# Two layers on one core: second- and third-pass tasks interleaved, the MLP's second product one step later

## What is computed

```python
# layer 0
tgt1 = _layer_norm(tgt, g1, be1)
tgt = tgt + _self_attn(tgt1, mask, Wq, bq, Wk, bk, Wv, bv, Wo, bo)
tgt = tgt + (memory @ Wg.T + bg)
tgt1 = _layer_norm(tgt, g2, be2)
x = tgt + jax.nn.relu(tgt1 @ W1.T + b1) @ W2.T + b2
# layer 1
x = mha(layer_norm(x, ln1_s, ln1_b), ..., causal=True) + x
y = mha(layer_norm(x, ln2_s, ln2_b), encoded, ..., causal=False) + x
z = layer_norm(y, ln3_s, ln3_b)
out = y + jax.nn.relu(z @ mlp_w1 + mlp_b1) @ mlp_w2 + mlp_b2
```

## Time and profile before

| | us |
|---|---|
| median of 3 runs | 1721.41 |
| lowest and highest | 1719.3, 1725.6 |
| the profiled execution | 1704.09 |
| its span, first to last instruction | 1702.3 |
| mean granted TensorE clock, share of full | 0.956 |

### The profile page before, as it was taken

How to read it: one execution, slowest core, us unless ns; L and a number is a source line. 1 busy time by engine, 2 the same in 40 slices (tenths; PEclk the granted TensorE clock), 3 DMA queues, 4 the chain that set the end, 5 groups by cost and what they waited for, 6 DMA issues and landing times.

```text
span 1702.3 us, 42833 instructions
## 1 busy us (share of the span) xinstructions
PE 1459.5 (86%) x13376; PEld 1175.9 (69%) x13376; DVE 1212.1 (71%) x3855; ACT 1061.9 (62%) x2153; POOL 834.7 (49%) x1125
## 2 busy tenths in 40 slices
PE   2789999999998998878787777778999999999986
PEld 1567788877777887765566555555777777777756
DVE  2688887888878887656666766666776777677742
ACT  3677676777777775445565555556656665666552
POOL 3345454444444566544344443444555655565533
PEclk8799999999999999989899999998999999999989
DMA  5645555444544455444655646574644364546300
GB/s 145 139 113 119 108 109 118 99 99 105 117 100 99 105 125 130 119 107 107 124 121 111 129 101 140 115 153 93 119 112 105 99 128 99 105 101 129 79 26 13
DMA packets 163511, 185.75 MB, mean 109 GB/s; under 512 B 15952, under 2 KB 140240, under 8 KB 163408
## 3 DMA queue, kind: packets, MB, share of 16 engines
q1 hardware_dynamic: 163408, 184.57, 49.8%
HBM read 125.78 MB, written 58.72 MB: 108 GB/s over the span
## 4 chain that ended last, share of the span: by engine, by line
PE 42%; issue 13%; ACT 12%; DVE 12%; DMA 9%; POOL 6%; SPq 5%; ACTq 1%; DVEq 0%; POOLq 0%
PE d_ps L437 16%; PE d_ps L673 8%; DMA k_stack<-parts 7%; PE o_ps L572 5%; PE s_ps L494 5%; PE t_ps L542 3%; DVE prob L858 3%; PE t_ps L508 3%; SPq L399 2%; DMA parts<-q_part 2%; ACT prob_t L721 2%; SPq L404 2%; DVE o_n L890 2%; POOL h_lo L1031 2%; PE m_ps L444 1%
## 5 line engine op out<-in xcount | busy, mean ns | idle before, releaser
L721 ACT ACTIVATE prob_t<-t_ps 128x384 f32<-128x384 f32 (+1 forms) x512 | 275.4, 551 | 393.0 <-PE t_ps L542 197.7
L494 PE MATMUL s_ps<-k_stack,q_stack 96*128 96x256 bf16 (+1 forms) x1536 | 294.6, 275 | 124.5 <-DMA k_stack<-parts 47.5
L712 ACT ACTIVATE prob<-prob,neg_max 128x256 f32<-128x256 f32 x512 | 233.8, 514 | 121.0 <-DVE neg_max L858 118.8
L494 PEld LDWEIGHTS s_ps<-k_stack,q_stack 96*128 96x128 bf16 x1536 | 115.1, 100 | 227.8 <-issue 65.7
L542 PE MATMUL t_ps<-q_stack,k_stack 108*128 108x256 bf16 (+1 forms) x1024 | 207.3, 269 | 23.0 <-ACT prob_t L721 14.3
L858 DVE CUSTOM_DVE_ANT_0 prob<-s_ps,bias_sb 128x256 f32<-128x256 f32 x512 | 192.4, 416 | 48.5 <-PE s_ps L494 36.7
L858 DVE CUSTOM_DVE_ANT_0 prob<-s_ps,causal 128x128 f32<-128x128 f32 (+1 forms) x512 | 158.5, 352 | 90.2 <-PE s_ps L494 88.0
L843 DVE TENSOR_REDUCE top<-s_ps 128x2 f32<-128x512 f32 x256 | 172.9, 682 | 54.8 <-PE s_ps L494 51.3
L1031 POOL TENSOR_TENSOR h_lo<-h_f,h_hi 128x512 fp32r<-128x512 f32 x128 | 165.9, 1296 | 86.6 <-DVE h_hi L921 86.6
L572 PE MATMUL o_ps<-prob_t,v_sb 128*17 128x256 f32 (+1 forms) x3072 | 200.7, 381 | 0.0
L437 PE MATMUL d_ps<-x2t_hi,w_hi 128*128 128x256 f32 x512 | 157.0, 307 | 38.2 <-ACT k_f L780 21.8
(11 more groups left out here) (115 smaller groups left out, 4063.5 us busy)
## 6 DMA issues: line engine op xcount, KB each, us to landing
q_stack<-parts SPq DMA_DIRECT2D x288, 128.0 KB, 4.0
k_stack<-parts SPq DMA_DIRECT2D x288, 128.0 KB, 6.4
parts<-q_part SPq DMA_DIRECT2D x96, 192.0 KB, 2.3
parts<-k_part SPq DMA_DIRECT2D x96, 192.0 KB, 2.3
ct_kept<-ct_hl SPq DMA_DIRECT2D x16, 512.0 KB, 8.0
x_in<-x_mid SPq DMA_DIRECT2D x32, 256.0 KB, 2.9
x_res<-x_mid SPq DMA_DIRECT2D x32, 256.0 KB, 3.0
ct_hl<-ct_kept SPq DMA_DIRECT2D x16, 512.0 KB, 8.2
```

Source lines behind the costliest of these rows:

```text
L494: last = mm(s_ps[:, h % 2, q * S:q * S + n], q_stack[0:ROWS, t.par, HEAD[h], q * P:(q + 1) * P], k_stack[0:ROWS, t.par, HEAD[h], 0:n], sta ...
L712: last = nc.scalar.activation(prob[:, h % 4, q, :], prob[:, h % 4, q, :], ACT.Exp, bias=neg_max[:, h % 4, q:q + 1], scale=-1.0)
L721: nc.scalar.activation(prob_t[:, h % 8, 0:n], t_ps[:, h % 2, 0:n], ACT.Exp, scale=-1.0)\
```

## The change

**Order.** Tasks 0 to 15 are the first pass as before, 16 to 19 are the first four of the second pass. From task 20 on a second-pass task (sequence 4 + b) and a third-pass task (sequence b) take turns, to task 43; the last four are third-pass tasks. `Task` and `Step` are rewritten for a list of the order, `steps` has two loops in place of three, and the counts that each semaphore wait is for are worked out from the list.

**Weights.** Second-pass q/k/v weights get tiles of their own (`wx_hi`, `wx_lo`), and its output weights lie where the gate weights were. So both passes' weights are on chip at once. The stage tile is gone: early units are staged where the MLP's and the output's tiles lie later (`late`), the others in the first pass's probability tile. Units are loaded and split at other steps: unit 4 at step 1 in place of 14, units 8 and 9 at steps 18 and 19 in place of 30 and 32.

**The second MLP product.** For a third-pass task that is followed by a second-pass one (`late()`) W2 runs one step later than before, in slots 5, 6 and 8, its sum in slot 9, and its store in slot 9.

**Masks.** The causal mask and its bf16 twin are made at step 15 in the tile of the first pass's mask. The guard of the second pass writes its shifted scores, which nobody reads, into one shared tile, and waits for the guard before it.

The diff, cut:

```diff
-           (14, 12): (4,), (16, 13): (5,), (17, 9): (6,), (17, 14): (7,), (30, 12): (8,), (32, 13): (9,)}
+           (1, 5): (4,), (17, 2): (5,), (17, 10): (6,), (17, 15): (7,), (18, 9): (8,), (19, 3): (9,)}
-UNIT_LOAD_AT = {(-2, 2): 0, (-1, 0): 1, (-1, 14): 2, (0, 5): 3, (1, 0): 4, (15, 0): 5, (17, 1): 6, (17, 11): 7,
-                (18 - 1, 15): 8, (31, 0): 9}
+UNIT_LOAD_AT = {(-2, 2): 0, (-1, 0): 1, (-1, 14): 2, (0, 5): 3, (0, 14): 4, (16, 6): 5, (17, 4): 6, (17, 12): 7,
+                (18, 1): 8, (18, 12): 9}
-GATE_AT, W2_AT = 12, (11, 12, 14)
+GATE_AT, W2_AT, W2_LATE = 12, (11, 12, 14), (5, 6, 8)
+LEAD = 4
+ORDER = ([(0, b) for b in range(B)] + [(1, b) for b in range(LEAD)]
+         + [t for b in range(B - LEAD) for t in ((1, LEAD + b), (2, b))] + [(2, b) for b in range(B - LEAD, B)])
...
+    def late(self):
+        return self.p == 2 and self.pos + 1 < NTASK and ORDER[self.pos + 1][0] == 1
...
+        self.w2 = None
+        if self.old and self.old.p in MLP and not self.old.late():
+            self.w2 = self.old
+        elif self.older and self.older.late():
+            self.w2 = self.older
...
+        wx_hi, wx_lo = sb("wx_hi", [P, 3, KC, D], F32R), sb("wx_lo", [P, 3, KC, D], F32R)
...
-                if h in W2_AT and has(st.old, MLP):
-                    part = W2_AT.index(h)
+                at = (W2_LATE if st.w2.late() else W2_AT) if st.w2 else ()
+                if h in at:
+                    part = at.index(h)
                     if part == 0:
-                        weights(st.old, UNIT_W2)
-                        pe.wait_ge(h_done.sem, h_done.after(st.old, 3))
+                        weights(st.w2, UNIT_W2)
+                        if st.w2.late():
+                            pe.wait_ge(k_done.sem, k_done.after(st.nxt))
+                        pe.wait_ge(h_done.sem, h_done.after(st.w2, 3))
...
+                if t.p == 1:
+                    dve.sem_inc(passed, 1)
+                    last, hb = earlier_head(st, h, 1)
+                    dve.wait_ge(u_done.sem, u_done.after(last, hb + 1))
...
+                    shifted = spill[:, q, 0:n] if t.p == 1 else prob[:, h % 4, q, 0:n]
+                    last = v.tensor_tensor_reduce(shifted, s_ps[:, h % 2, q * S:q * S + n], bias,
...
-                if h == 15 and has(st.old, MLP):
-                    dve.wait_ge(w2_mm.sem, w2_mm.after(st.old))
+                if st.w2 and h == y_at(st.w2):
+                    t, before = st.w2, st.mlp_before(st.w2)
+                    dve.wait_ge(w2_mm.sem, w2_mm.after(t))
```

More of the change, by code:

```diff
@@ L104, in __init__, with mlp_before @@
         self.prev, self.old, self.older = at(-1), at(-2), at(-3)
+        self.w2 = None
[3 more added lines that the diff above has]
+            self.w2 = self.older
+    def mlp_before(self, task):
+        pos = task.pos - 1
+        while pos >= 0 and ORDER[pos][0] not in MLP:
+            pos -= 1
+        return Task(pos, task.i) if pos >= 0 or task.i is not None else None
 def steps(eng, body):
-    for s in range(-2, 2):
+    for s in range(-2, PAIRS_0):
@@ L119 @@
+    for s in range(NTASK - LEAD - 3, NTASK + 2):
+        body(Step(s))
 class Event:
@@ L144, in after @@
     def after(self, task):
[L146 to L148 removed]
+        n = sum(p in self.passes for p, _ in ORDER[task.par:task.pos + 1:2]) if task.pos >= 0 else 0
+        const = 16 * (self.dmas * n + self.credit)
+        return task.i * (16 * self.dmas) + const if task.i is not None and task.p in self.passes else const
 def two_layers(nc, x, ctx, mask, wa, wm1, wm2, cols, rows, ident, out):
@@ L193, in two_layers @@
         ident_bf = sb("ident_bf", [P, P], BF16)
-        later = sb("later", [P, P], BF16)
         one_hot = sb("one_hot", [P, CH])
@@ L545, in keyed_scores @@
                     if t.p == 1:
-                        last = mm(t_ps[:, h % 2, k * S:k * S + P], ident_bf[:, :], later[:, :], start=False, stop=True)
+                        last = mm(t_ps[:, h % 2, k * S:k * S + P], ident_bf[:, :], later, start=False, stop=True)
                 last.then_inc(st_mm.sem, 1)
@@ L799, in slot @@
                     act.wait_ge(w1_mm.sem, w1_mm.after(st.old, n + 1))
+                    if st.old.first and n == 0:
+                        act.wait_ge(unit_lo, 5)
                     if n >= 2:
```

236 lines of the change are left out of this document (134 added, 102 removed).

## The result

The changed kernel is slower: a median of 1739.1 us against 1717.0 us of the kernel before on the same chips, a ratio of 1.0118 with a 95% interval of 1.009 to 1.0145. The prediction, 1700 us, was wrong in its direction. Four of the changed kernel's 17 runs were over 1.5% above its fastest; they are in its median and not in the ratio.

A forecast was written before the change was run, and what follows sets the result against it. Second-pass steps were taken as ended by the k_stack transfer, third-pass steps as bound by TensorE. Terms of 800.4, 79.9, 618.0 and 182.9 us made a span of 1681.2, 21 less, hence a median of 1700 us; range 1664 to 1727.

The forecast's parts named there:

- What bounds the kernel before: Second-pass steps (27.0 us) end in a wait for the k_stack transfer; third-pass steps (34.0 us) are bound by TensorE.
- TensorE work: TensorE's busy time at full clock in the alternating steps: 25.3 us in A, 26.3 us in B.
- Idle time that B keeps: TensorE's idle time in B, built from the MLP-free step 1118.8 to 1144.7: 5.8 - 2.5 - 1.7 + 0.8 us.
- B: Alternating step whose current task is a third-pass one; forecast 28.7 us, 29.0 with the transfer's 0.3.
- Idle time that A keeps: TensorE's idle time in A: 2.1 + 0.8 + 0.7 us of waits and 0.7 for the layer norm.
- A: Alternating step whose current task is a second-pass one; forecast 29.6 us, 29.9 with the transfer's 0.3.
- The sum: Whole span: 800.4 us, steps 20 to 22 79.9, steps 23 to 43 618.0, the end 182.9; total 1681.2 us.
- the rival on the transfer: Transfer ends both kinds of alternating step and TensorE's clock falls: x = 31.2 us, total 1738 us; chance 0.14.
- x: Mean length of the 21 alternating steps, 23 to 43; the forecast's own range was 28.7 to 30.0 us.
- The transfer in B and A: Loads land 24.6 to 30.2 us into a step; late ones poke out by up to 1.4; 0.3 us a step added.
- The guard's added wait: Second-pass score guards, each waiting for the guard before: 0.1 us a step, bounds 0 and 54 us in all.
- Weights: Weight splits moved to steps 1, 18 and 19 hold GpSimd: 5 us taken, bounds 0 and 7.9 us.

The follow-up runs named there:

- b2: Kernel before with 44 of the 48 products of the third pass's second MLP product left out (output not the reference's); 1722.4 us, ratio 1.0014.
- d1: b2 with 16 products whose result nobody reads in slot 11 of third-pass steps; 1709.1 us, ratio 0.9961 to the kernel before.
- e3: Changed kernel with products nobody reads in slot 11 of steps 23 to 44, 10 in A and 16 in B; 1729.8 us, ratio 1.0074.
- e2: Changed kernel with one layer-norm normalisation on VectorE moved from slot 10 to slot 11; 1746.8 us, ratio 1.0189 to the kernel before.
- e4: Changed kernel with the late second MLP product in slots 9, 11 and 12 of A in place of 5, 6 and 8; 1744.5 us, ratio 1.0174.
- c1: Changed kernel with the first layer norm's statistics and variance moved from slots 9 and 10 to 4 and 5, steps 23 to 44; 1701.6 us, ratio 0.9918.
- f1: c1 with input normalisation in slot 9 (was 12), transposes in 11 (13), ScalarE's copies in 12 (14), steps 23 to 44; 1692.7 us, ratio 0.9866.
- b1: Kernel before with each second-pass score guard waiting for the guard before it, and nothing else; 1722.2 us, ratio 1.0029.
- b3: Kernel before with the first layer norm's statistics and variance moved from slots 9 and 10 to 4 and 5 in all steps; 1731.8 us, ratio 1.0071.
- d2: Kernel before with 16 products whose result nobody reads at the end of slot 15 in the second pass; 1709.0 us, ratio 0.9974.
- e1: Changed kernel with the second MLP product back in its old slots 11, 12 and 14, tasks still alternating; 1722.3 us, ratio 1.0041.
- c2: c1 with products nobody reads in slot 11 of steps 23 to 44, 6 in A and 5 in B; 1702.6 us, ratio 0.9933.
- f4: Changed kernel with ScalarE's four affine copies of the input in slot 13 in place of 14, steps 23 to 44; 1758.2 us, ratio 1.0235.
- f3: c1 with f1's edits and with weight splits moved to later slots; 1689.5 us, ratio 0.9838 to the kernel before.

## Why the prediction was wrong, by its steps

**What bounds the kernel before: right.** Second-pass steps ended in the transfer, and the change removed that: 25.8 us became 1.9.

**TensorE work: right.** 25.3 and 26.3 us forecast, 25.4 and 26.2 measured.

**Idle time that B keeps: the step that failed.** 2.4 us forecast, 5.0 measured. After the K copy (0.8 taken, 0.60 measured) 1.6 us were left for all the rest, read off the step at 1118.8:

```profile
1134.77 0.17 DVE L874 TENSOR_SCALAR ve<-mv 128x2 f32<-128x2 f32 x1
```

```profile
1135.59 0.39 PE L494 MATMUL s_ps<-k_stack,q_stack 96*128 96x256 bf16 x2 [0.54 <-DVE top L843]
1137.93 0.39 PE L494 MATMUL s_ps<-k_stack,q_stack 96*128 96x256 bf16 x2 [0.74 <-DVE top L843]
```

That step has no MLP at all: no activation to split, so no GpSimd instruction beside the variance add, which took 0.17 us, and no casts between the maxima. It also began behind a wait for the transfer, so that the one for the exponentials in slot 0 didn't show. B has them, and 3.3 us of waits in slots 12 and 13 (2.32, 0.74 and a last 0.25), besides 1.10 us in slot 0. The text said that W2 "covered VectorE's work there" and gave no price to it. The price is in b2 and d1: of 5.2 us of W2 1.1 come back at full clock, and none where the clock falls. In B itself TensorE has 5.8 us less to do than in the third-pass step (26.2 against 32.0), and at full clock B is 2.8 us shorter. The step to start from was the third-pass step of 34.0 us with all of VectorE's work of slots 9 to 13 laid end to end, and not one that lacks part of that work.

**Idle time that A keeps: about right, in other places.** 4.3 us (and 0.3 for the DMA) forecast, 4.9 measured. Slots 11 to 13 have 2.26 where 2.1 was taken; slot 0 has 1.29 for 0.74; the layer norm's 0.7 didn't come, and a wait of 0.77 for a `q_stack` copy in slot 15 did. The K copy cost 0.28 us where 0.8 was taken. That the sum came out within 0.6 us is in part luck: the terms' errors cancel.

**The sum.** At full clock these make 646.2 us for 23 to 43, against 618.0 forecast: 28.2 of the 46.7 us by which the span missed. The clock's 10.7 (below) and 7.8 outside these steps are the rest.

**The clock: it had no term.** It stood only in the rival on the transfer. The 21 steps cost 10.7 us more than at full clock; in e3's execution, with more work, they were 8.8 us shorter. In e2 and e4 the same products took 18.6 and 14.4 us more than in the changed kernel, with less idle time. The rival's second half, that waits of TensorE bring the lower clock, was right, and its first, that the transfer makes the waits, wrong: x came out at 31.3, its 31.2, and its total, 1738 us, is about 1 us from the median, by another way. The sign for "wrong" that the text gave for it, k_stack waits in nearly every step, wasn't there.

**The transfer in B and A: right only for the longer steps.** One wait of 1.9 us in 21 steps, where 0.3 us a step were taken. But c1, whose steps are nearer to the forecast's, has 21.6 us of such waits, 1.0 a step. The reading was at fault: 3.4 to 9.0 us is the range of all six k_stack loads, and a step waits for the last of the six. Taken step by step in the same rows, the last takes 4.4 to 9.0 us, over 8 in six of the eleven steps, and it lands 25.6 to 30.5 us in, 28.4 on average, where the text has 27.4. The length of the steps doesn't settle it alone: f1's are shorter than c1's (617.5 us against 624.1) and have 5.3 us of these waits.

**The guard's added wait:** too small to be told from nothing (b1), as forecast. **Weights:** 5 us taken; step 1 took 2.6 us longer than before and steps 16 to 19 together 2.1, so about right, 4.7, although the other first-pass steps gave 2.5 back in that execution (steps 0 to 15: 613.7 and 613.6).

**The rest of the span.** The first scores start 4.2 us later; but b1, b2, b3, d1 and d2, whose start is the old one, have 43.2 to 45.5 us as well, so most of it is the luck of the one execution before, with 41.3. Steps 20 to 22 took 84.1 us against 79.9 forecast; kernels with after's code in these steps (e1, e3, e4, c1, c2, f1, f4) take 84.0 to 88.0 there, those with before's (before, b2, d1) 79.1 to 84.0, and b1, with the guard's wait alone, 87.0. So part of it may be the change's after all, and what it is wasn't settled. Step 44 to the end took 185.5 us against 182.9 forecast.

**The forecast's mean was reachable.** f3's 21 steps take 618.5 us, the 618.0 of the sum, once VectorE's and ScalarE's pieces are placed for the new order. That the two agree so closely is chance: its A and B are 28.4 and 30.8 us, not 29.9 and 29.0. But the sum described a kernel whose other engines had been moved along with TensorE.

## What to carry to other kernels

Work that stands in front of another engine's burst is cover: before it is moved, lay out what that engine must do in its slots, for the new step and not for a similar one, because taking the work away may save a fifth of its length or nothing (b2, d1). Price each wait of a busy TensorE twice, for itself and for the clock after it. When an order of tasks is changed, put the side engines' work where the new waits are not, in the same change; here that alone turned 1.0118 into 0.9866 (f1).

## What the runs showed of the hardware

After waits of TensorE of no more than 0.7 to 2.3 us the granted clock fell from 2.4 to 1.2 GHz for part of a step: a B of 31.2 us at full clock took 34.0 at 0.90 (after, step 37), and one of 35.8 stood at 0.81 (e2). Step 33, with the same waits as step 37, ran at 1.00 throughout; what decides between the two isn't shown here. The Trainium skill describes such a case ("TensorE: Matmul & The Clock Gate", A second HAM failure mode: psum-queue depth-cycling): frequent short idles between groups of products make the clock go back and forth. The trace agrees, and shows what it is worth: the same products of the 21 steps keep TensorE busy for 563.3 us at 0.96 (after) and for 581.9 at 0.92 (e2), and with 26 useless products a pair, run inside the waits, the clock was 0.99 and the steps were 8.8 us shorter (e3).
